# Graph counts in a fused layer: the transposed counts of a tile are applied three tiles later, not two

## The reference

```python
def _L0_gnn_ref(x, edge_src, edge_dst, w, W1, W2, W3):
    agg = jax.ops.segment_sum(x[edge_dst], edge_src, num_segments=N_NODES)
    y = agg + w * x
    h = jax.nn.relu(jnp.einsum('nd,hd->nh', y, W1))
    h = jax.nn.relu(jnp.einsum('nh,gh->ng', h, W2))
    h = jax.nn.relu(jnp.einsum('ng,og->no', h, W3))
    return h + x

x = x + _L0_gnn_ref(_layernorm(x, axis=-1), src, dst, ...)
x = x + _L0_ffn_ref(_layernorm(x, axis=-1)[None], ...)[0]   # top 2 of 8 experts
```

## Time and profile before

| | us |
|---|---|
| median of 3 executions | 530.05 |
| lowest, highest | 529.33, 532.99 |
| the profiled execution | 532.43 |
| its span | 530.6 |
| PE busy, share of the span | 394.8, 74% |
| DVE busy, share of the span | 308.6, 58% |

### The profile page before, as it was taken

The page is one execution under the profiler, slowest core; times in us unless marked ns, Lnnn a source line. Parts: engine busy times, 40 slices in busy tenths (PEclk is TensorE's granted clock), DMA queues, the critical chain, the costliest instruction groups (busy, mean ns, idle before and its releaser), DMA issues.

```text
span 530.6 us, 12803 instructions
## 1 busy us (share of the span) xinstructions
PE 394.8 (74%) x4336; PEld 355.9 (67%) x4337; DVE 308.6 (58%) x712; ACT 216.2 (41%) x336; POOL 157.7 (30%) x247
## 2 busy tenths in 40 slices
PE   1307765687888886889842499999999999999500
PEld 1306644677887876676742399999999999999400
DVE  5739859757778760455469544444444444444664
ACT  2204315456666664265610254444444354444000
POOL 2158513000000000000000446666666656663300
PEclk9957555889999999988755599999999999999855
DMA  7622006779989899599110112222222222121989
GB/s 178 154 81 50 0 5 112 123 139 173 182 164 173 164 179 180 161 367 338 51 48 0 51 50 80 65 75 69 69 69 69 69 69 79 62 76 51 268 192 294
DMA packets 112754, 63.43 MB, mean 120 GB/s; under 512 B 86333, under 2 KB 106601, under 8 KB 112602
## 3 DMA queue, kind: packets, MB, share of 16 engines
q1 hardware_dynamic: 102388, 43.93, 37.2%
q0 software_dynamic: 7072, 16.00, 9.7%
q10 hardware_dynamic: 3270, 3.20, 1.7%
HBM read 28.76 MB, written 13.85 MB: 80 GB/s over the span
## 4 chain that ended last, share of the span: by engine, by line
PE 53%; DMA 20%; DVE 10%; issue 5%; SPq 5%; ACT 3%; POOL 1%; ACTq 0%; DVEq 0%; POOLq 0%
PE psum L871 18%; PE psum L882 17%; DMA at<-cts 14%; PE psum L743 4%; PE psum L790 3%; PE psum L812 3%; PE psum L734 2%; SPq L281 2%; PE psum L860 2%; DMA w_sb<-pair_rows 2%; PE psum L689 2%; DMA edge_key<-key_f 1%; DMA pair_rows<-yb,scol 1%; PE psum L800 1%; DVE rounds_f L1016 1%
## 5 line engine op out<-in xcount | busy, mean ns | idle before, releaser
L871 PE MATMUL psum<-xgT,w_now 128*128 128x128 f32 x832 | 103.6, 279 | 0.0
L561 ACT CAST cts<-psum 128x1000 bf16<-128x1000 f32 x100 | 78.4, 814 | 57.1 <-PE psum L734 57.0
L871 PEld LDWEIGHTS psum<-xgT,w_now 128*128 128x128 f32 x832 | 99.3, 195 | 0.2 <-issue 0.2
L882 PE MATMUL psum<-w_sb,hT 128*128 x416 | 98.4, 380 | 0.0
L743 PE MATMUL psum<-z,at 125*128 (+1 forms) x1875 | 74.8, 197 | 23.9 <-DMA at<-cts 23.9
L743 PEld LDWEIGHTS psum<-z,at 125*128 125x128 bf16 x1875 | 67.8, 100 | 28.9 <-issue 19.8
L882 PEld LDWEIGHTS psum<-w_sb,hT 128*128 128x128 f32 x416 | 75.1, 190 | 8.4 <-issue 0.3
L647 ACT ACTIVATE hT<-up 128x512 f32<-128x512 f32 x52 | 32.7, 630 | 100.0 <-DVE up L1295 100.0
L470 POOL COPY gcol<-gidx 128x1 int32 (+1 forms) x52 | 9.6, 187 | 210.2 <-DVEq L1260 210.2
L636 ACT COPY w_now<-w_sb 128x1024 f32 x52 | 54.4, 1045 | 32.8 <-DVEq L1260 21.9
L488 POOL DMA_INDIRECT pair_rows<-yb,scol x52 | 51.6, 992 | 47.5 <-issue 34.2
(11 more groups left out here) (219 smaller groups left out, 390.9 us busy)
## 6 DMA issues: line engine op xcount, KB each, us to landing
w_sb<-in_L_ffn_W_dram SPq DMA_DIRECT2D x2, 4096.0 KB, 20.7
res<-in_x_dram SPq DMA_DIRECT2D x5, 560.0 KB
token_rows<-tok SPq DMA_DIRECT2D x5, 560.0 KB
tok<-pair_rows SPq DMA_DIRECT2D x5, 560.0 KB
w_sb<-pair_rows SPq DMA_DIRECT2D x5, 560.0 KB
out_dram<-res ACTq DMA_DIRECT2D x5, 560.0 KB
b_sb<-in_L_ffn_b_dram SPq DMA_DIRECT2D x1, 1024.0 KB, 24.2
xg<-token_rows,gcol POOLq DMA_INDIRECT x52, 2.8
```

The lines of the kernel that those rows point to most:

```text
L561: act.copy(cts[:, par, :, d0:d0 + nw * WD].rearrange("p h (b d) -> p b h d", b=nb), psum[:, bank:bank + nb, 0:wb * WC].rearrange("p b (d h ...
L871: last = pe.matmul(psum[:, j % 2, c * P:(c + 1) * P], w1_now[:, j % 2, k, c * P:(c + 1) * P], xgT[:, j % 2, k, :], start=(k == 0), stop=(k ...
L882: last = pe.matmul(psum[:, 4 + j % 2, 0:D], hT[:, j % 2, k, :], w2_sb[:, ds(e, 1), k, :].rearrange("p a h -> p (a h)"), start=(k == 0), st ...
```

## The change

PE's program alone changes. The applies of tile kt-3 and not kt-2 stand in slot kt; in the first three tiles there are windows alone; behind the last window follow the applies of three tiles. What SP, ACT and DVE do and wait for has the same code as before.

```diff
                 for kt in range(NBUF):
                     for c in range(NC):
                         window(kt, kt, c, kt == 0 and c < 2)
-                        if kt >= 2:
-                            apply(kt - 2, 0, kt - 2, c)
 
                 def tile(kt, i, par):
                     for c in range(NC):
                         window(kt, par, c, False)
-                        apply(kt - 2, i if par == 2 else i - 1, (par + 1) % NBUF, c)
+                        apply(kt - NBUF, i - 1, par, c)
 
                 later_tiles(pe, tile)
-                for kt in (NT - 2, NT - 1):
+                for kt in range(NT - NBUF, NT):
                     for c in range(NC):
                         apply(kt, kt // NBUF, kt % NBUF, c)
```

## The result

| | before | after |
|---|---|---|
| median, us | 531.52 (4 runs) | 514.37 (4 runs) |
| lowest, highest | 529.33, 536.23 | 513.62, 515.64 |
| the profiled execution | 532.43 | 513.81 |
| its span | 530.6 | 511.9 |

The ratio is 0.9668, with a 95% interval of 0.9595 to 0.9742: 17 us faster. The forecast was 511.0, its range 508 to 520.

A forecast was written before the change was run, and what follows sets the result against it. The prediction took a latency loop of two tiles, 4.79 us a tile, as the bound, with SP's issue next at 4.15; 3.79 us at the start plus 15.25 in the stretch gave 19.0 saved: median 511.0, range 508 to 520.

The forecast's parts named there:

- The latency loop of two tiles: Transposition, apply two slots later, copies, next transposition: 9.58 us per two tiles, 4.79 a tile, bounds the kernel before.
- SP's queue as the next bound: SP issues one transposition at a time, 3.79 us each plus gaps: 12.44 us per three tiles, 4.15 a tile.
- The second rival: The DMA engines bound at the share shown: 4.41 us a tile, 5.2 us more in all, 516; chance 0.13.
- The size of the gap: Pause between two issues on SP's queue: 0.28 us when nothing is awaited, 0.51 at the loop's branch.
- Issues held up: Issue times from the fourth transposition on: 3.83, 4.08, then 19 x 3.79 us, within a stretch of 87.4.
- the third rival: Back-to-back issues on SP's queue are slower, 4.49 us, 4.85 a tile; total 525.3, within 1%; chance 0.08.
- The start: Slot 2 no longer waits for transposition 0; third and fourth issues come 3.79 us earlier, at 96.06 and 100.96.
- Slack: Three tiles of issues take 12.44 us, the latency loop of three tiles needs 9.58: 2.9 us to spare.
- The fourth rival: The change does nothing, as SP's turn(kt) waits for its own slot's end and gives back the tile: 530; chance 0.04.
- The end: Last transposition issued at 188.4, last matmuls end 9.18 us after it as before; the extra apply costs nothing.
- my rival for slower: PE's new waits let its granted clock drop: 1% slower from 8 of 22 tiles, some 578 if all; chance 0.05.
- The signs: PE's landing waits no fewer but shorter; SP's copy wait nearly gone; issues 4.07, 4.07, 4.30 us apart; DMA share 1.05.

The follow-up runs named there:

- e2: Changed kernel with PE's old wait for the landing of transposition kt-2 put back, new apply order kept: median 531.7 us, ratio 0.996 to the kernel before.
- e7: Kernel before, with each transposition moving only 20 of 25 blocks, as many matmuls: 520.8 us, ratio 0.979 to the kernel before.
- e5: Changed kernel with SP's loop over the tiles written out 25 times, other engines unchanged: 512.2 us, ratio 0.962 to the kernel before.
- e6: e5, plus PE's last apply share ahead of the last window part and SP's second wait removed: 511.2 us, ratio 0.959 to the kernel before.
- e1: The changed kernel run again, unaltered, as the measure for the runs beside it: 516.7 us, ratio 0.970 to the kernel before.
- e11: The changed kernel run again, unaltered, beside e9 and e10: 516.3 us, ratio 0.968 to the kernel before.
- e3: Changed kernel with only the start's wait put back, PE in slot 2 waiting for transposition 0: 518.2 us, ratio 0.974 to the kernel before.
- e4: Changed kernel with four buffers in place of three and applies four tiles behind: 521.1 us, ratio 0.979 to the kernel before.
- e9: e6 plus filler matmuls on PE at the stage's end, 36 before the last applies and 16 behind: 511.0 us, ratio 0.959 to the kernel before.
- e10: e6 run again, unaltered, beside e9 and e11: 510.8 us, ratio 0.957 to the kernel before.
- e8: Changed kernel with each transposition moving only 20 of 25 blocks, as many matmuls: 504.5 us, ratio 0.946 to the kernel before.

## Why the prediction was right, step by step

**The latency loop of two tiles** was the bound: shown, by e2, which brings the 9.57 us back with the wait alone, and by e7, which shortens the landing and gets the loop shorter by just that.

**SP's queue as the next bound**: shown, by e5 and e6. The Trainium skill, Perfetto Trace Analysis, section What "DMA-bound" means, names this bound; the trace agrees, with SP's queue held or between two issues for the whole of the stretch. The second rival, the share of the 16 engines, falls: the share is 1.02 after and 1.11 at 205 GB/s in e6, over a window of 50 us. A share of 0.92 had been no limit. The time alone would not have told: that rival's 516 is where e1 and e11 came out (516.7, 516.3).

**The size of the gap was the term that was mis-sized.** I read 0.28 us between two issues, where nothing is awaited, at the first and second transposition (0.25 in fact: the second starts at 91.27, which the view rounds to 91.3). These are written out, with constants for the tile; in the loop the same step is 0.38 or 0.39, and at the branch 0.67 to 0.70 and not 0.51. The branch is passed six times, not seven; the last gap, behind the loop, is 0.44. The 21 gaps add up to 9.9 us, where 7.5 were forecast: 2.4 us too little. The row that gave 0.51 has the same fault: it stands between the part written out and the loop. e5 shows it from the other side, by writing the rest out.

**Issues held up.** I had put 3.83 and 4.08 for the fourth and fifth, from before; they took 4.29 and 4.37, and one near the end 4.37: 1.3 us more, and 0.2 over the other 18. With the 2.4 this makes the 3.9 us by which the stretch from the fourth to the 25th issue (98.51 to 189.86, 91.3) exceeds the 87.4 of the sum. Back-to-back issues are not slower as a rule (the third rival): in the steady stretch they took 3.73 to 3.86.

**The start.** Fourth issue after the first: forecast 14.6 us, measured 13.5, mostly because the first and third issue took 4.31 and 3.79 us and not 4.64 and 4.39. e3 prices the wait that went at 2.3 us.

**Slack.** Of 2.9 us, forecast for the wait for `applied` and the loop of three tiles, the trace shows 3.2: the slot with the applies of the transposition issued at 129.41 ends its copies at 139.01 (136.86 + 2.15, timeline of after), and SP gets to that tile's issue at 142.23. The fourth rival (the wait gives all back) falls with it, and e4 shows that more depth has nothing to add.

**The end.** 9.18 us from the last issue to the last apply were forecast, 8.8 us measured (189.86 to 198.64). The extra tile of applies lies ahead of the landing that PE waits for (timeline of after, then the last two tiles):

```profile
188.12 2.36 PE L743 MATMUL psum<-z,at 125*128 125x64 bf16 x75 [2.42 <-DMA at<-cts]
192.54 6.10 PE L743 MATMUL psum<-z,at 125*128 125x64 bf16 x150 [2.06 <-DMA at<-cts]
```

**The clock**, my rival for slower, stayed at 1.00 (2.4 GHz) through the stretch. It fell to 0.50 at 193.2, in the last 150 matmuls, much as it had in the kernel before.

**The signs.** PE's waits for landings became shorter but also fewer, 14 and not 22, where I had said as many or more. SP's wait for copies fell to the first one, the issues lie 4.1 to 4.3 us apart, and 4.5 across the branch (4.07, 4.07 and 4.30 forecast), and the DMA share is 1.02 (1.05).

The parts of the whole: the stage 16.5 us shorter (130.6 to 114.1), where 19.0 was the sum: 1.1 more at the start, 3.9 less in the stretch, 0.4 more at the end. The profiled execution came to 513.8, where the prediction has 513.4; that is luck, as its span is 18.7 us shorter only because it also began its stage 1.4 us earlier and had 0.8 less behind it. The median, 3.4 us above the forecast, shows the miss.

## What to carry to other kernels

A loop of a long wait and a short body costs its latency divided by the number of tiles it spans: read the chain, count the tiles between two links, and compare with what every engine needs for a tile, queues that only issue DMAs among them. Depth pays until the next of these prices is reached and nothing after (e4), and then the work between two issues is what is left to cut (e5, e6). A gap must be read at the same kind of instruction that will stand there: a step with constants is not the price of the same step in a loop.

## What the runs showed of the hardware

- SP's queue was held by a transposition nearly in proportion to its blocks: 3.79 us for 25, 3.06 for 20, some 0.15 us a block.
- Between two issues on SP, nothing awaited: 0.67 to 0.70 us at a loop's branch, 0.38 in a loop with two waits, 0.27 with a constant tile number, 0.16 with one wait. Single gaps were longer in the kernels with SP written out (0.77 in e5, 0.62 in e6, e9 and e10, always at the same tile in these three); why was not looked into.
- Some issues took 4.0 to 5.0 us and not 3.8, in every run with all 25 blocks, mostly among the first five and the last two. Which ones changed from profile to profile of the same kernel (the second took 4.41 in after, 3.82 in e1). The cause was not found and not tried.
- The stage behind took 79.4 to 84.1 us with the same instructions, and its granted clock went with it: over the first 30 us behind y the mean was 0.90 or 0.91 in the five profiles with 79.4 to 79.9 us, 0.89 in e9 (80.9), 0.83 in e2 and e3 (81.7), 0.77 in e4, e6, e8 and e10 (83.0 to 84.1). Only e11 stands apart (0.90 and 83.2): its clock fell later, to 0.67 where after had 0.84, from 30 to 40 us behind y. The changed kernel itself shows both ends (79.4 in the first profile, 83.2 in e11), which fits the spread of 6 us between its runs. Where the clock stood in the tail of the stage does not decide it. It had fallen there and was back for y in before, after, e1, e3, e4, e5, e9 and e11, with 79.4 to 84.1 us behind y; it stayed at 1.00 through the tail in e2, e6, e7, e8 and e10, with 79.7 to 83.0. What does decide it stays open.
